# Attention in a fused layer: the products with the values in one wide block a step, and the order of scores and maxima around it

## The reference

```
q, k, v = heads of rmsnorm(x) @ wq.T, wk.T, wv.T     # 16 heads of 16, 8 batches, 1024 tokens
scores  = q @ k.T * 0.25
probs   = softmax(scores, axis=-1)
out     = probs @ v, then @ wo.T, added to x
```

## Time and profile before

| what | value |
|---|---|
| median of three runs | 2974.03 us (2972.51 to 2976.35) |
| the profiled execution | 2974.94 us, span 2973.2 us |
| mean granted TensorE clock | 0.963 |
| instructions in the profile | 62637 |
| PE busy | 2850.3 us, 96% of the span |
| PE weight loads (PEld) | 1785.6 us, 60% |
| DVE busy | 2266.5 us, 76% |
| ACT busy | 1815.3 us, 61% |
| POOL busy | 690.2 us, 23% |

### The profile page before, as it was taken

The page is one execution under the profiler, slowest core; times in us unless marked ns, Lnnn a source line. Parts: engine busy times, 40 slices in busy tenths (PEclk is TensorE's granted clock), DMA queues, the critical chain, the costliest instruction groups (busy, mean ns, idle before and its releaser), DMA issues. The chain is left out here.

```text
span 2973.2 us, 62637 instructions
## 1 busy us (share of the span) xinstructions
PE 2850.3 (96%) x22877; PEld 1785.6 (60%) x22878; DVE 2266.5 (76%) x4076; ACT 1815.3 (61%) x3460; POOL 690.2 (23%) x996
## 2 busy tenths in 40 slices
PE   5999999979999999999999999989888999999997
PEld 4777777753333333333333333347677888888886
DVE  5777877749999999999999999957795555555553
ACT  3666666635888888888888888875442222222221
POOL 2223322321000000000000000001104555555554
PEclk8999999987999999999999999998889999999999
DMA  1233333332222222222222222227642333333332
GB/s 47 100 115 114 114 114 114 107 128 63 83 74 80 65 74 69 62 74 70 65 69 75 66 65 74 60 60 226 203 156 40 52 50 51 51 50 51 50 51 38
DMA packets 170750, 243.12 MB, mean 82 GB/s; under 512 B 30920, under 2 KB 118240, under 8 KB 170512
## 3 DMA queue, kind: packets, MB, share of 16 engines
q1 hardware_dynamic: 121920, 170.57, 18.8%
q0 software_dynamic: 31152, 52.33, 9.1%
q10 hardware_dynamic: 17440, 16.98, 1.8%
HBM read 126.53 MB, written 111.21 MB: 80 GB/s over the span
## 5 line engine op out<-in xcount | busy, mean ns | idle before, releaser
L1065 DVE TENSOR_REDUCE b_mxq<-b_p_m 128x1 f32<-128x1024 f32 x1024 | 1220.2, 1221 | 77.3 <-PE b_p_m L1092 68.2
L999 ACT ACTIVATE b_probs<-b_p_e 128x512 f32<-128x512 f32 x2048 | 1105.4, 597 | 141.5 <-PE b_p_e L1145 40.3
L1092 PE MATMUL b_p_m<-b_kst,b_qst 64*128 64x512 f32 x1536 | 568.7, 450 | 0.8 <-DVE b_mxq L1065 0.8
L1145 PE MATMUL b_p_e<-b_qst,b_kst 64*128 64x512 f32 x1536 | 559.6, 444 | 0.2 <-ACT b_probs L999 0.2
L1117 PE MATMUL b_p_o<-b_probs,b_vst 128*32 128x256 f32 x6160 | 482.3, 391 | 0.5 <-ACT b_probs L999 0.4
L1145 PEld LDWEIGHTS b_p_e<-b_qst,b_kst 64*128 64x128 f32 x1536 | 236.3, 184 | 312.4 <-ACT b_probs L999 266.0
L1886 ACT COPY d_hT<-d_p_h 128x512 f32<-128x512 f32 x136 | 79.8, 587 | 401.7 <-PE d_p_h L1979 401.7
L1117 PEld LDWEIGHTS b_p_o<-b_probs,b_vst 128*32 128x32 f32 x6160 | 126.3, 108 | 243.6 <-issue 131.0
L1856 POOL DMA_INDIRECT out_dram<-d_y,d_to x136 | 217.6, 1600 | 200.9 <-PE d_p_x L1964 116.1
L1987 PE MATMUL d_p_y<-w2T,d_hT 128*128 x1088 | 257.1, 379 | 1.5 <-ACT d_hT L1886 1.5
L1092 PEld LDWEIGHTS b_p_m<-b_kst,b_qst 64*128 64x128 f32 x1536 | 234.5, 186 | 15.7 <-DVE b_mxq L1065 12.4
(11 more groups left out here) (314 smaller groups left out, 4482.8 us busy)
## 6 DMA issues: line engine op xcount, KB each, us to landing
b_qst<-qk_d SPq DMA_DIRECT2D x288, 64.0 KB
b_kst<-qk_d SPq DMA_DIRECT2D x288, 64.0 KB
qk_d<-a_hi SPq DMA_DIRECT2D x32, 512.0 KB, 2.8
qk_d<-a_lo SPq DMA_DIRECT2D x32, 512.0 KB, 3.8
v_d<-a_v_s SPq DMA_DIRECT2D x16, 1024.0 KB, 4.9
o_d<-b_oT POOLq DMA_DIRECT2D x63, 256.0 KB, 2.7
b_vst<-v_d SPq DMA_DIRECT2D x48, 256.0 KB
raw<-in_L_ffn_w_dram SPq DMA_DIRECT2D x24, 512.0 KB, 4.8
```

The source lines that it names most:

```text
L999: nc.scalar.activation(probs[(2 * step + e % 4 // 2) % BUFS][:, (e % 2) * 512:(e % 2 + 1) * 512], p_e[(slot(e) if more1 else e) % EB][:], ...
L1065: V_.reduce_max(mxq[half][:, h, qt:qt + 1], p_m[j % 2][:], AX.X).then_inc(s["m_red"], 1)
L1092: mm(p_m[j % 2][:, kh * 512:(kh + 1) * 512], qst[r][rows(h), qt * P:(qt + 1) * P], kst[r][rows(h), kh * 512:(kh + 1) * 512], start=True, s ...
L1145: mm(p_e[u % EB][:], kst[r][rows(h), kt * P:(kt + 1) * P], qst[r][rows(h), a * 512:(a + 1) * 512], start=True, stop=True).then_inc(s["e_ps ...
```

## The change

`values` loses its `part`: one call makes the whole step, with four matmuls of 512 columns in place of eight of 256. Its waits for the exponentials and for `oT_done` stand ahead of the whole block, and its count of `pv_done` follows the last of the four. In the order, `value(n)` is now step n, still counted from the last step of the pair before. Each line of the order has one step: four scores and four halves of maxima (two units) in a row, and then one whole block of values. The warm-up matmuls on `p_o` ahead of the first pair become four of 512 columns, and the last step after the last pair is one block.

```diff
-        def values(step, part):
+        def values(step):
 
             pair, kt = step // KT, step % KT
-            if part == 0:
-                pe.wait_ge(s["e_done"], pair * SLOTS + (slot(4 * kt + 3) if pair < PAIRS - 1 else 4 * kt + 3) + 4)
-            if kt == 0 and part == 0:
+            pe.wait_ge(s["e_done"], pair * SLOTS + (slot(4 * kt + 3) if pair < PAIRS - 1 else 4 * kt + 3) + 4)
+            if kt == 0:
                 pe.wait_ge(s["oT_done"], pair + 1)
-            at = 256 * part
             for h in range(2):
                 for a in range(2):
-                    last = mm(p_o[32 * (2 * h + a):32 * (2 * h + a) + 32, at:at + 256], vst[step // KT % RING][:, step % KT, h, :],
-                              probs[(2 * step + h) % BUFS][:, a * 512 + at:a * 512 + at + 256], start=(step % KT == 0 and part == 0), stop=(step % KT == KT - 1), skip_group_check=True)
-            if part == 1:
-                last.then_inc(s["pv_done"], 1)
+                    last = mm(p_o[32 * (2 * h + a):32 * (2 * h + a) + 32, :], vst[pair % RING][:, kt, h, :],
+                              probs[(2 * step + h) % BUFS][:, a * 512:a * 512 + 512], start=(kt == 0), stop=(kt == KT - 1), skip_group_check=True)
+            last.then_inc(s["pv_done"], 1)
...
-                values(pair * KT - 1 + n // 2, n % 2)
+                values(pair * KT - 1 + n)
...
             scores(0); maximum(0); maximum(1); scores(1); scores(2); maximum(2); scores(3); maximum(3); value(0)
-            scores(4); maximum(4); value(1); scores(5); maximum(5); maximum(6); scores(6); maximum(7); scores(7); value(2); value(3)
-            scores(8); maximum(8); maximum(9); scores(9); value(4)
-            scores(10); maximum(10); maximum(11); scores(11); value(5)
...
-            scores(22); maximum(22); maximum(23); scores(23); turned(); value(11)
...
-            scores(30); maximum(30); maximum(31); scores(31); value(15)
+            scores(4); maximum(4); maximum(5); scores(5); scores(6); maximum(6); maximum(7); scores(7); value(1)
+            scores(8); maximum(8); maximum(9); scores(9); scores(10); maximum(10); maximum(11); scores(11); value(2)
...
+            scores(20); maximum(20); maximum(21); scores(21); scores(22); maximum(22); maximum(23); scores(23); turned(); value(5)
...
+            scores(28); maximum(28); maximum(29); scores(29); scores(30); maximum(30); maximum(31); scores(31); value(7)
```

More of the change, by code:

```diff
@@ L1134, in _ @@
         pe.wait_ge(s["start"], 1)
-        for part in range(2):
-            for g in range(4):
-                mm(p_o[32 * g:32 * g + 32, part * 256:part * 256 + 256], vst[RING - 1][:, 0, 0, :], probs[BUFS - 2][:, 0:256], start=(part == 0), stop=False, skip_group_check=True)
+        for g in range(4):
+            mm(p_o[32 * g:32 * g + 32, :], vst[RING - 1][:, 0, 0, :], probs[BUFS - 2][:, 0:512], start=True, stop=False, skip_group_check=True)
         def body(pair, i, r, more1, more, more3):
@@ L1162, in body @@
             scores(0); maximum(0); maximum(1); scores(1); scores(2); maximum(2); scores(3); maximum(3); value(0)
-            scores(4); maximum(4); value(1); scores(5); maximum(5); maximum(6); scores(6); maximum(7); scores(7); value(2); value(3)
-            scores(8); maximum(8); maximum(9); scores(9); value(4)
-            scores(10); maximum(10); maximum(11); scores(11); value(5)
[L1166 to L1170, removed]
-            scores(22); maximum(22); maximum(23); scores(23); turned(); value(11)
-            scores(24); maximum(24); maximum(25); scores(25); value(12)
-            scores(26); maximum(26); scores(27); maximum(27); value(13)
-            scores(28); maximum(28); scores(29); maximum(29); value(14)
-            scores(30); maximum(30); maximum(31); scores(31); value(15)
+            scores(4); maximum(4); maximum(5); scores(5); scores(6); maximum(6); maximum(7); scores(7); value(1)
+            scores(8); maximum(8); maximum(9); scores(9); scores(10); maximum(10); maximum(11); scores(11); value(2)
+            scores(12); maximum(12); maximum(13); scores(13); scores(14); maximum(14); maximum(15); scores(15); value(3)
+            scores(16); maximum(16); maximum(17); scores(17); scores(18); maximum(18); maximum(19); scores(19); value(4)
+            scores(20); maximum(20); maximum(21); scores(21); scores(22); maximum(22); maximum(23); scores(23); turned(); value(5)
+            scores(24); maximum(24); maximum(25); scores(25); scores(26); maximum(26); maximum(27); scores(27); value(6)
+            scores(28); maximum(28); maximum(29); scores(29); scores(30); maximum(30); maximum(31); scores(31); value(7)
         pairs(pe, body)
-        for part in range(2):
-            values(PAIRS * KT - 1, part)
+        values(PAIRS * KT - 1)
 class ProjectionTiles:
```

## The result

The changed kernel takes 3049.98 us (median of four runs, 3047.5 to 3051.94) against 2973.27 us for the kernel before, measured beside it: a ratio of 1.0262, 95% interval 1.0248 to 1.0276. The forecast was 3055 us, in a range of 2998 to 3080. The profiled execution of the changed kernel has a span of 3050.2 us, 77.0 more than before.

The account below looks back on a forecast made before the run. PE's order of time was taken as the bound. Eight strides of 2.61 us plus 0.17 and 0.26 make a pair 21.31 against 20.05; 64 x 1.26 = 81 us on 2974 gives 3055 us, range 2998 to 3080.

Parts of the forecast that it names:

- What bounds: In the attention, PE's order of time sets the pace, 20.04 of 20.06 us a pair; DVE and ACT could go faster.
- Width: Block of values on PE: four wide products take 1.00 us to the next score, as two halves did; no gain.
- Fewer switches: PE switches to one block of values a step instead of two: without any wait 2.12 us against 2.46, 0.34 gained.
- The wait: With three score banks, each step's fourth score waits for its first score's exponential: at 1.18 us, not 0.80, losing 0.38.
- the cold products: Products on PE behind the score that waited start 0.43 us after it, not 0.32.
- The six plain strides: Steps of a pair (four scores, one block of values) without an extra late start: 2.61 us each, 0.15 above 2.46.
- The second stride: Second step of a pair: its products wait for ACT's copy of the outputs after exponential 4, 0.17 us more.
- The sixth stride: Sixth step of a pair: the transpose of the maxima waits for exponential 21, products at 1.87 not 1.61, 0.26 more.
- The sum: Whole attention: a pair takes 21.31 us against 20.05, 64 x 1.26 = 81 us more.
- A: Rival, chance 0.05: the fourth score does not wait, PE's step is 2.12 us, DVE sets 2.26; 112 us less, 2862 us.
- B: Rival, chance 0.08: the waiting score's weights load during its wait, products follow in 0.32; 24 us more, 2998 us.
- C: Rival, chance 0.04: PE's new gaps of 0.4 us take its clock down; 3100 us.

## Why the prediction was right

The time came out 5 us under the 3055 forecast, and by the path that the forecast named: the loop through score, exponential and fourth score. Point by point, from the changed kernel's order in time beside the forecast:

- **What bounds.** PE's order, with DVE and ACT able to go faster: right. The order before gained 26 us with four banks and short reductions, where the new order gained 227 (3049.98 to 2823.18), and 7 with short exponentials, where the new order gained 103.
- **Width.** Nothing, right: 3048.45 us with halves, 3049.98 with whole blocks. A block takes 0.99 to 1.00 us to the next score in both.
- **Fewer switches.** 0.34 a stride: right, and seen by itself in the run with four banks (2.12 against 2.46).
- **The wait.** 1.18 forecast, 1.18 to 1.19 measured; the cold products 0.43 forecast, 0.42 to 0.43 measured. The six plain strides average 2.61, as forecast. The whole of the answer was in the kernel before, in the first four scores of each pair.
- **The second stride.** 2.78 forecast, 2.74 to 2.75 measured, and here the nearness is luck: two sizes were wrong and nearly cancel. The copy does not wait for the end of exponential 4; it starts 0.49 after its start, as the next exponential would. And the products start 0.15 after the copy's end, not 0.05; why is not shown:

```profile
1338.35 0.60 ACT L999 ACTIVATE b_probs<-b_p_e 128x512 f32<-128x512 f32 x1 [0.55 <-PE b_p_e L1141]
1338.84 0.58 ACT L989 COPY b_oT<-b_p_o 128x512 f32<-128x512 f32 x1
```

```profile
1337.82 0.50 PE L1141 MATMUL b_p_e<-b_qst,b_kst 64*128 64x512 f32 x1
...
1339.57 1.06 PE L1115 MATMUL b_p_o<-b_probs,b_vst 128*32 128x512 f32 x8
1340.56 0.50 PE L1141 MATMUL b_p_e<-b_qst,b_kst 64*128 64x512 f32 x1
```

  In the earlier trace rows the copy, at 1203.28, did follow the end of its exponential. There it also stood behind the old pair's second half of products, which it waits for in the code and which by their row ended at 1203.21; the forecast read that as ACT's own spacing:

```profile
1202.57 0.64 PE L1117 MATMUL b_p_o<-b_probs,vst 128*32 128x256 f32 x8
```

- **The sixth stride.** 2.87 forecast, 2.89 measured (1348.38 to 1351.27), the transpose at 1.68 (1.66 forecast) and the products 0.21 behind it, as forecast:

```profile
1348.38 0.50 PE L1141 MATMUL b_p_e<-b_qst,b_kst 64*128 64x512 f32 x1
...
1350.06 0.28 PE L1098 MATMUL b_p_e<-b_ident,b_hl 128*32 128x128 f32 x1
1350.27 1.06 PE L1115 MATMUL b_p_o<-b_probs,b_vst 128*32 128x512 f32 x8
1351.27 0.49 PE L1141 MATMUL b_p_e<-b_qst,b_kst 64*128 64x512 f32 x1
```

- **The sum.** 81 us forecast, 77 measured in the median. A pair is 21.26 and not 21.31, and the period before is 20.06 and not 20.05: 1.20 for 1.26 on most pairs, some 4 us in all. The last interval between copies grew by only 0.5 us (18.07 to 18.55), 0.8 less than the forecast charged it.
- **The rivals.** A did not come, since its condition, the exponential done by 0.75, did not hold; where a fourth bank took the condition away, the stride fell to the 2.12 it names for PE. The rule of the Trainium skill that a change of tiling mode drains TensorE ("TensorEngine Tiling (Array Packing)", Key Properties) agrees with the rows: products follow a score after 0.32, another score follows after 0.23. It did not decide. B did not come: the waiting score's weights are loaded after the wait (the PEld row at 1341.74), not during it. C did not come: the clock is 1.00 with 0.4 us gaps in every stride.

## What to carry to other kernels

Fusing work into fewer, longer blocks saves switches, but it puts the same kind of instruction in a row, and in this kernel a row longer than its ring of buffers waits inside the row for the consumer's whole round trip. Count the row against the ring on every engine that it feeds, and look in the old trace for a place where that row already stands: it gives the price without an estimate. If the ring can't grow, the short blocks in between are what hides the round trip. Giving the scores' ring a bank of the maxima's, with all maxima kept, only moved the wait.

## What was not expected of the hardware

ACT starts the next instruction 0.49 us after one of 0.60 us even where the two differ in kind, an exponential and then a copy, so an end read from one row is not when the next can start. A reduction of 512 columns starts 0.61 us after the one before it, of 1024 columns 1.13, so cutting one in two costs DVE 0.09 us. And the maxima's ring of three cost more than the scores' ring of three: 2.73 us a stride against 2.61.
